# Four graph layers on one core: VectorE's spread operands in PSUM, and the third layer's loads on another queue

## What is computed

```python
x = x + gat(h)        # softmax over a node's edges and its own loop of leaky_relu scores; weighted sum of h @ W
x = x + sage2(h)      # mean of h[src] by dst -> 64 -> relu -> mean again -> 32
x = x + symmetric(h)  # features 16 to 31 summed over neighbours in both directions, / degree; 32 -> 128 -> relu -> 32
x = x + relations(h)  # sum over edges of tanh(relu(score)) * (w_comp[type] @ bases)(h[src]); self loop at the last edge
```

## Time and profile before

| | |
|---|---|
| median of 3 runs | 5175.08 us (5169.4 to 5180.67) |
| the profiled execution's own time | 5181.43 us |
| its span on the core | 5179.2 us |
| busy: GpSimd (POOL) | 3688.3 us, 71% |
| busy: VectorE (DVE) | 2956.8 us, 57% |
| busy: TensorE (PE), weight loads (PEld) | 2376.9 us, 1415.0 us |
| busy: ScalarE (ACT) | 934.8 us, 18% |
| DMA | 327.77 MB, mean 63 GB/s |

### The profile page before, as it was taken

How to read it: one execution, slowest core, us unless ns; L and a number is a source line. 1 busy time by engine, 2 the same in 40 slices (tenths; PEclk the granted TensorE clock), 3 DMA queues, 4 the chain that set the end, 5 groups by cost and what they waited for, 6 DMA issues and landing times. The chain is left out here.

```text
span 5179.2 us, 30233 instructions
## 1 busy us (share of the span) xinstructions
PE 2376.9 (46%) x8870; PEld 1415.0 (27%) x8870; DVE 2956.8 (57%) x3467; ACT 934.8 (18%) x1345; POOL 3688.3 (71%) x3150
## 2 busy tenths in 40 slices
PE   7800166664777730000523320466665556556563
PEld 3400033332444420000523320122221333333331
DVE  8864266665777745555423221255554677787785
ACT  0011011111344421111000000233332111111110
POOL 8777777763777747776688888775561577777775
PEclk9955555555889875555555555677877777777786
DMA  1043234441344422222122222333332000110100
GB/s 26 10 134 113 53 79 85 88 88 48 133 137 144 137 96 59 59 62 63 5 5 5 5 5 5 97 115 123 128 116 89 24 27 23 30 28 22 29 23 14
DMA packets 347732, 327.77 MB, mean 63 GB/s; under 512 B 223247, under 2 KB 295834, under 8 KB 346364
## 3 DMA queue, kind: packets, MB, share of 16 engines
q1 hardware_dynamic: 102512, 267.39, 14.6%
q0 software_dynamic: 144256, 45.62, 8.8%
q10 hardware_dynamic: 100800, 12.85, 2.0%
HBM read 170.38 MB, written 156.58 MB: 63 GB/s over the span
## 5 line engine op out<-in xcount | busy, mean ns | idle before, releaser
L1326 POOL DMA_INDIRECT sum_table<-e_add_rows,e_add_idx x392 | 655.7, 1673 | 174.1 <-issue 118.9
L522 POOL DMA_INDIRECT g_ring<-x_table,pos x392 | 440.8, 1125 | 226.0 <-issue 119.2
L522 POOL DMA_INDIRECT c_ring<-x_table,pos x392 | 456.3, 1164 | 199.6 <-issue 127.0
L522 POOL DMA_INDIRECT d_ring<-g_table,pos x392 | 436.5, 1114 | 178.9 <-issue 124.0
L522 POOL DMA_INDIRECT f_ring<-con_table,pos x392 | 401.4, 1024 | 222.7 <-issue 118.3
L1673 POOL DMA_INDIRECT out_x<-g_out_rows,end_index x392 | 424.3, 1082 | 185.5 <-issue 119.3
L522 POOL DMA_INDIRECT b_ring<-h_table,src x392 | 425.1, 1085 | 162.0 <-issue 118.7
L332 POOL DMA_INDIRECT x_dst<-in_x,dst x392 | 444.6, 1134 | 132.6 <-issue 132.6
L1843 PE MATMUL g_pX<-w,g_h_T 128*128 128x512 f32 x784 | 440.0, 712 | 128.0 <-DVEq L1707 128.0
L1587 PE MATMUL f_pH<-f_T,w2in 128*128 128x448 f32 x672 | 344.8, 662 | 306.2 <-DVE f_T L1492 306.2
L1373 PE MATMUL e_pS<-e_values,e_equal 128*128 128x17 f32 x784 | 168.8, 374 | 419.3 <-DVEq L1346 419.3
(11 more groups left out here) (331 smaller groups left out, 5212.3 us busy)
## 6 DMA issues: line engine op xcount, KB each, us to landing
f_sums<-sum_table SPq DMA_DIRECT2D x126, 238.0 KB, 4.0
sum_table<-c_zero SPq DMA_DIRECT2D x39, 715.0 KB, 5.4
g_table<-c_g SPq DMA_DIRECT2D x42, 448.0 KB, 2.5
g_etype<-in_etype_rows SPq DMA_DIRECT2D x14, 1204.0 KB
h_table<-a_xp SPq DMA_DIRECT2D x28, 560.0 KB, 3.3
a_x<-in_x SPq DMA_DIRECT2D x28, 448.0 KB, 5.8
b_h_node<-h_table ACTq DMA_DIRECT2D x28, 448.0 KB, 4.8
b_x_node<-in_x SPq DMA_DIRECT2D x28, 448.0 KB, 3.5
```

The costliest lines, as they stand in the source:

```text
L522: pool.indirect_dma_start(out=ring[:, t, :], out_offset=None, in_=table, in_offset=bass.IndirectOffsetOnAxis(ap=idx[:, c * C + t:c * C + t ...
L1326: pool.indirect_dma_start(out=g.sums[b], out_offset=bass.IndirectOffsetOnAxis(ap=aidx[:, c % 2, t:t + 1], axis=0), in_=add[:, c % 2, t, :] ...
```

## The change

`Norm.space` now also makes `bank`, a PSUM tile of one bank (512 numbers per partition; in every stage the call is `space()`, so the bank is in PSUM). The sums of the rows and the inverse roots stand in its first 112 numbers, and each stage takes further columns for its own spread operands. Where such an operand was a slice of an SBUF tile, a `tensor_copy` of 28 or 32 numbers per chunk brings it into the bank; where it was computed, the computation writes there (`rden`, `rdeg`, the inverse). In attention the carried numerator is read from PSUM where it lies. In second SAGE the gathered values by feature, `gm`, move from SBUF to PSUM. `g.before` in symmetric, and L1388 there, stay as they were.

```diff
     @contextmanager
-    def space(self):
+    def space(self, bank=True):
...
+            make = self.nc.psum_tensor if bank else self.nc.sbuf_tensor
+            self.bank = ctx.enter_context(make(f"norm{self.spaces}_bank", [P, 512 if bank else Norm.USED], f32))
...
-        nc.vector.tensor_reduce(self.stat[:, s, 0, :], x, AX.X, ALU.add)
+        nc.vector.tensor_reduce(self.mean(n), x, AX.X, ALU.add)
         dve.drain()
-        nc.vector.scalar_tensor_tensor(out=self.xc[:, s], in0=bc_feat(self.stat[:, s, 0, :]), scalar=-1.0 / F, in1=x,
+        nc.vector.scalar_tensor_tensor(out=self.xc[:, s], in0=bc_feat(self.mean(n)), scalar=-1.0 / F, in1=x,
...
@@ attention, values
+                nc.vector.tensor_copy(weight, ex[:, 0, :])
+                nc.vector.tensor_copy(own_weight, ex[:, 1, :])
                 dve.drain().then_inc(d_ready, 1)
...
-                nc.vector.tensor_tensor(val[:, 0:F, :], swap(ring[:, a, :, 0:F]), bc_tile(ex[:, 0, :], F), ALU.mult)
+                nc.vector.tensor_tensor(val[:, 0:F, :], swap(ring[:, a, :, 0:F]), bc_tile(weight, F), ALU.mult)
...
@@ third layer, fill
-                nc.vector.tensor_tensor(ends[:], swap(x), bc_tile(g.end[:, part(c)], F), ALU.mult)
+                nc.vector.tensor_copy(end, g.end[:, part(c)])
+                dve.drain()
+                nc.vector.tensor_tensor(ends[:], swap(x), bc_tile(end, F), ALU.mult)
...
@@ third layer, SyncE's loop over the jobs
-                if j + 2 < J:
-                    sp.wait_ge(turned, j + 1)
-                    load(j + 2)
                 sp.wait_ge(x3_ready, j + 1)
...
@@ third layer, ScalarE
             def hidden(j, ns):
                 for n in ns:
+                    if n == 0 and j + 2 < J:
+                        act.wait_ge(turned, j + 1)
+                        load(j + 2)
...
                 out(j)
+                hidden(j + 1, range(2, 8))
+                out(j + 1)
                 if c:
                     act.wait_ge(filled, c)
                 nc.scalar.copy(more[:], bc_tile(g.more0[:, part(c)], F)).then_inc(more_set, 1)
-                hidden(j + 1, range(2, 8))
-                out(j + 1)
                 hidden(j + 2, range(8))
...
@@ relations
-        pT = pb("pT", 2)
...
-                    if c or k:
-                        pe.wait_ge(turned_sb, c * 2 + k)
-                    pe_quads(nc, pT, h[k], g.ident[:], turned)
+                    if c:
+                        pe.wait_ge(bases_used, c * D - 1 + k)
+                    pe_quads(nc, pX[k], h[k], g.ident[:], turned)
```

More of the change, by code:

```diff
@@ L103 @@
 class Norm:
+    USED = 4 * C
     def __init__(self, nc, g):
@@ L132, in spread @@
         dve.wait_ge(self.squared, n + 1)
-        self.nc.vector.tensor_reduce(self.stat[:, s, 1, :], self.sq[:, s], AX.X, ALU.add).then_inc(self.summed, 1)
+        self.nc.vector.tensor_reduce(self.stat[:, s, 0, :], self.sq[:, s], AX.X, ALU.add).then_inc(self.summed, 1)
     def scale(self, dve, n):
         dve.wait_ge(self.rooted, n + 1)
-        self.nc.vector.reciprocal(self.stat[:, n % 2, 3, :], self.stat[:, n % 2, 2, :])
+        self.nc.vector.reciprocal(self.inverse(n), self.stat[:, n % 2, 1, :])
         dve.drain()
@@ L552, in stage_attention @@
         prow = pm[0:K1, 2 * P:3 * P]
+        at = Norm.USED
+        watt = w.bank[:, at:at + 3 * F].rearrange("p (k f) -> p k f", f=F)
+        weight, own_weight, rden = (w.bank[:, at + 3 * F + k * C:at + 3 * F + (k + 1) * C] for k in range(3))
         rows = [SW("rows0"), SW("rows1")]
@@ L1166, in stage_sage_second @@
         pm = ctx.enter_context(nc.psum_tensor("d_pm", [P, 512], f32))
-        pc = ctx.enter_context(nc.psum_tensor("d_pc", [P, 512], f32))
+        pc = pm[:, 256:512]
+        gm = ctx.enter_context(nc.psum_tensor("d_g_by_feature", [P, 1024], f32))[:, 0:F * C].rearrange("p (f t) -> p f t", t=C)
+        share, end = (w.bank[:, Norm.USED + k * C:Norm.USED + (k + 1) * C] for k in range(2))
         pall = ctx.enter_context(nc.psum_tensor("d_pall", [P, 2048], f32))
@@ L1265, in _ @@
                 act.wait_ge(rows[c % 2], GAT * (c // 2 + 1))
-                nc.scalar.copy(gm[:], swap(ring[:, c % 2])).then_inc(ring_free, 1)
+                if c:
+                    act.wait_ge(cr.owned, c)
+                nc.scalar.copy(gm, swap(ring[:, c % 2])).then_inc(ring_free, 1)
                 w.root(act)
@@ L1427, in _ @@
             g.sem.clear_before(sp)
[L1428 to L1432, removed]
             def load_node(k):
@@ L1436, in load_node @@
                 sp.dma_start(flat(radn[:, k % 2]), node_rows(g.RN, k, CON)).then_inc(n_here[k % 2], 16)
-            for j in range(2):
-                load(j)
-                load_node(j)
+            for k in range(2):
+                load_node(k)
             for j, (kind, k) in enumerate(jobs):
-                if j + 2 < J:
-                    sp.wait_ge(turned, j + 1)
-                    load(j + 2)
                 sp.wait_ge(x3_ready, j + 1)
@@ L1547, in _, with load @@
         def _(act):
+            def load(j):
+                kind, k = jobs[j]
+                for i, table in enumerate(g.sums):
+                    frm = edge_rows(table, k, CW) if kind == "e" else node_rows(table, k, CW, base=EPAD)
+                    act.dma_start(sums[:, j % 2, i].rearrange("p t f -> p (t f)"), frm).then_inc(here[j % 2], 16)
             def hidden(j, ns):
                 for n in ns:
+                    if n == 0 and j + 2 < J:
+                        act.wait_ge(turned, j + 1)
+                        load(j + 2)
                     act.wait_ge(hid_done, j * 8 + (n + 1))
@@ L1558, in out @@
                 nc.scalar.activation(osb[:].rearrange("p (h k) -> p h k", h=2), pO[:].rearrange("p (h k) -> p h k", h=2)[:, :, 0:HALF], ACT.Identity, bias=g.b2out[:, 0:1]).then_inc(out_sb, 1)
+            for j in range(2):
+                load(j)
             for c in range(EC):
@@ L1691, in x_full @@
             def x_full(c):
-                sum_back(nc, dve, g, g.x_in[:, c, :], g.by_feature(c), c, xf[:])
+                nc.vector.tensor_copy(after, g.x_in[:, c, :])
+                dve.drain()
+                sum_back(nc, dve, g, after, g.by_feature(c), c, xf[:])
                 dve.drain()
```

56 lines of the change are left out of this document (37 added, 19 removed).

## The result

The change takes 4973.71 us (median; 4972.45 to 4980.69), the kernel before, run beside it, 5174.86 (5169.4 to 5180.67). The ratio is 0.9612, with a 95% interval of 0.9600 to 0.9623: 201 us less. The profiled execution of the change took 4980.69 us, its span 4979.0, so the spans differ by 200.2 us.

What follows compares the result with a forecast made beforehand. GpSimd's indirect DMAs were taken to bound second SAGE and nearly first SAGE, a VectorE-TensorE-ScalarE chain third layer. Terms -41, -20, -10, -3, -138, -8 sum to -220: 4961 profiled, median 4955, range 4885 to 5030.

Steps and rivals of the forecast that it cites:

- The lock: VectorE products with two SBUF operands hold up GpSimd's gathers and scatters; an operand in PSUM frees them.
- the slower rival: Full-width instructions with spread operands from PSUM run at half rate, 0.78 us more each: 5212 us, chance 0.04.
- Second SAGE: GpSimd bounds this stage; releasing 4.3 of 6.5 us of locking per chunk gives -41 us, between 28 and 52.
- First SAGE, tables, symmetric: Forecast -20 (limited by VectorE's removable waits), -10 (only norms released) and 0 us (large product stays in SBUF).
- The term of -3: Attention: two added copies cost 4.7 us, a faster strided product gives 10.9, partly beside TensorE; between -8 and +6.
- if only the pairing of two SBUF streams makes it slow, L653 falls to 1.09: Attention's strided product drops from 1.866 to 1.09 us with its spread operand in PSUM, giving 10.9 us.
- only VectorE's own time counts: In attention gathers wait for VectorE's chain, so freeing GpSimd was given no gain there.
- Third layer, the mask: Copying the fill mask behind the second job's output cuts VectorE's 6.9 us wait to about 0.3: -6.6 per chunk.
- Third layer, the sums: Loading sums from ScalarE's queue removes 3.9 of a 10.12 us wait per chunk; the radial load then comes late.
- the ends' product: Third layer's strided product, with one copy added, was to give -4 us; the load issues take 3 back.
- The rival that third layer gains all: The radial load is there at once and the whole 10.12 us goes: 20 to 30 us more, 4930, chance 0.17.
- Relations: Forecast -8 us, between -21 and +8; VectorE's loop through edge types bounds most chunks, and type waits cover the transposes.

Runs made afterwards that it cites:

- bank_sbuf2: The change with the bank of spread operands as an SBUF tile in place of PSUM, same instructions and order; 5044.09 us, ratio 0.9744.
- sym_psum: The change with symmetric's large comparison written to and read from PSUM, and ScalarE copying it for TensorE; 4941.18 us, ratio 0.954.
- strides: The change with three strided instructions altered: attention's product made a plain strided copy, two other products unstrided, some values wrongly ordered; one execution, 4960.52 us.
- mask_only: The kernel before with only the third layer's fill mask copied behind the second job's output; 5084.81 us, ratio 0.9837.
- radial_early: The change with the third layer's radial load issued ahead of the stores, on its own semaphore; 4968.31 us, ratio 0.9596.
- third_only: The kernel before with the third layer's later mask copy and sums loaded from ScalarE's queue, spread operands left in SBUF; 5057.78 us, ratio 0.9779.
- types2: The change with the edge types of relations loaded and spread in two parts, the first one earlier; 4927.97 us, ratio 0.9522.

## Why the prediction was right, and where it was not

The forecast of 4955 was 19 us too fast, within its range.

- **The lock.** Right, and shown: bank_sbuf2 gives back the delays with the same instructions, and sym_psum removes the last large one (44 us in its stage, 33 in the median). No full-width product without a stride is above 1.1 us with an operand in PSUM, which removes the slower rival.
- **Second SAGE.** -41 forecast, -43.8 measured, gathers at 1.002 us for the forecast 1.01. The split was near as well: the scan had 1.2 of 4.3 parts, 11 us; measured 7.3. The same code took 567.8 to 581.6 us in other kernels, so part of the closeness is luck.
- **First SAGE, tables, symmetric.** -18.0, -7.4 and +1.4, within 3 us of their terms. That first SAGE stops when VectorE's waits are used up agrees with the fall from 72.7 to 30.1. For tables only the sign is sure.
- **Attention.** The term of -3 had a wrong content. The step "if only the pairing of two SBUF streams makes it slow, L653 falls to 1.09" failed: 1.865. The rule I weighed against it, of the Trainium skill, SBUF — State Buffer, section "Door 1: The DMA port swizzle", that an access crossing to another 16-byte line pays, foretold this; strides agrees with it: two other products fall to 1.09 us without their stride. By it the stage would have lost 5 us. It lost none (-0.9), because a second step failed: "only VectorE's own time counts" in attention. With the bank in SBUF the stage is 4.6 us longer, so GpSimd's release counts there too; VectorE's time counts as well, since strides takes 0.84 us from each of 14 values and its attention is 14.6 us shorter (637.3).
- **Third layer, the mask.** -6.6 per chunk forecast, 7.1 measured by mask_only.
- **Third layer, the sums.** The new wait stands where it was put, with another size. I let the radial half land 4.0 us after its issue, so 3.9 of 10.12 would go. In the change VectorE starts 5.5 us after the issue in the mean, 1.5 later; the same sum with 5.5 gives 2.4 per chunk, and the edit gives 2.3. This is the term that was mis-sized: the forecast was 86 for the mask, 51 for the sums, 4 for the ends' product less 3 for issues, 138; measured are 92.1, 29.4 and 3.4 for all the rest, 124.9. The 4 for the ends' product had no ground: it took 1671 ns before and takes 1714, as the stride would have it. The chunk that I read, 50.7 us, was also longer than the mean of 49.4; the forecast period of 39.4 came out as 40.3.
- **The rival that third layer gains all** priced the radial wait at 20 to 30 us, since GpSimd stops it. radial_early gave 5 to 14 for taking the wait away. What bounds the chunk was right, its room too large: GpSimd needs 39 us, not 37 to 38, since once VectorE is denser its gathers are locked more often (1070 ns against 1024).
- **Relations.** -8 forecast, -6.7 measured, but the same code spreads over 9 us here, and with the bank in SBUF the stage is 1168.4. The near hit is luck. Two effects of the change stand in the stage. From one chunk's scatters to the next's it takes 78.2 us where it took 80.0 (79.2 and 79.7 in mask_only and third_only), but near the end, from the third-last chunk's scatters to the second-last's, it takes 78.0 where it took 66.2. With the bank in SBUF the two figures are 78.5 and 77.6, so neither comes from the operands' place, and what causes them stays open. That the type waits were the loop's bound failed for the middle of the stage: without 12.8 us of them a chunk there is 0.9 us shorter, and VectorE waits 122.7 us for rows instead, so GpSimd's pace is next; what types2 gave beyond 10 us came at the ends.

## What to carry to other kernels

Where GpSimd makes descriptors all the time, look in the timeline for those that end just after a VectorE instruction with two operands in SBUF. A copy of 28 numbers into PSUM (0.18 us), from where the spread operand is read, frees GpSimd during a 1.09 us product. It pays where GpSimd is the bound or near it: 44 us in second SAGE, 18 in first SAGE, nothing in the third layer. A wait's total is no estimate of what removing it gives: 111 us gave 5 to 14, 163 gave 46, and in the third layer and the middle of relations the other engine's pace, read from its group as count times mean plus gap, set the limit. When a load is moved ahead, ask at once which other load of the same job still stands behind the old store.

## What was not expected of the hardware

- A step of 28 to 40 elements makes a full-width VectorE instruction with two operands take 1714 to 1865 ns, where 1081 to 1088 suffice without it, even if the other operand is in PSUM, and on the input side (L669, L1532) and the output side (L153) alike.
- The work of one engine makes the other's transfers longer when it is packed closer: with no edit to gathers or products, mask_only's third layer has gathers of 1075 ns where before had 1024.
